# A relational graph layer: the first chunks in pieces, five halves by quarters, the bias spread by TensorE

## The reference

```python
masks = (relation[None] == rel_ids[:, None, None, None]).astype(x.dtype)
h = jnp.einsum('rbnm,bmd->rbnd', masks, x)
y = jnp.einsum('rbnd,rdo->bno', h, weight)
out = layernorm(x + y + bias)          # over the last axis
```

## Time and profile before

| what | value |
|---|---|
| three runs, median | 139.17 us (138.47 to 139.57) |
| profiled execution | 138.68 us |
| its span in the trace | 136.9 us |
| PE busy | 124.1 us, 91% |
| DVE busy | 85.8 us, 63% |
| ACT busy | 83.0 us, 61% |
| POOL busy | 69.2 us, 51% |
| DMA, mean over the span | 309 GB/s |

### The profile page before, as it was taken

How to read it: one execution, slowest core, us unless ns; L and a number is a source line. 1 busy time by engine, 2 the same in 40 slices (tenths; PEclk the granted TensorE clock), 3 DMA queues, 4 the chain that set the end, 5 groups by cost and what they waited for, 6 DMA issues and landing times.

```text
span 136.9 us, 2235 instructions
## 1 busy us (share of the span) xinstructions
PE 124.1 (91%) x727; PEld 77.2 (56%) x727; DVE 85.8 (63%) x270; ACT 83.0 (61%) x85; POOL 69.2 (51%) x79
## 2 busy tenths in 40 slices
PE   5986799489999999999999999999999999997920
PEld 2355688346564747465565656565656474666810
DVE  1185213765758494958677675757585939488851
ACT  3655753379785848484848586777758484513040
POOL 3000019975295709680786259553957195405440
PEclk9999999999999999999999999999999999999985
DMA  4999969999999999999999999999913000300422
GB/s 125 415 427 418 427 230 419 421 426 414 426 426 406 423 421 421 420 423 417 412 419 424 414 424 424 424 412 414 382 59 158 0 0 0 153 0 0 160 77 84
DMA packets 7789, 42.24 MB, mean 309 GB/s; under 512 B 864, under 2 KB 1376, under 8 KB 3936
## 3 DMA queue, kind: packets, MB, share of 16 engines
q1 hardware_dynamic: 7776, 42.08, 75.3%
HBM read 37.88 MB, written 4.19 MB: 307 GB/s over the span
## 4 chain that ended last, share of the span: by engine, by line
PE 73%; DMA 15%; SPq 4%; ACT 2%; DVE 1%; issue 1%; POOL 1%
PE h_ps L194 54%; DMA adj_sb<-in_adj_dram 15%; PE y_ps L201 10%; PE tp_ps L178 9%; ACT mask L171 1%; SPq L152 1%; SPq L258 1%; SPq L155 1%; POOL scale L219 1%; ACT h_sb L392 0%; DVE out_sb L223 0%; DVE stats L207 0%; ACT out_sb L398 0%; SPq L270 0%; SPq L269 0%
## 5 line engine op out<-in xcount | busy, mean ns | idle before, releaser
L171 ACT ACTIVATE mask<-adj_sb 128x2048 fp8e4<-128x2048 int32 x30 | 57.2, 1906 | 9.0 <-DMA adj_sb<-in_adj_dram 9.0
L194 PE MATMUL h_ps<-maskT,x_sb 128*128 128x512 fp8e4 (+1 forms) x152 | 32.0, 352 | 3.5 <-DVE maskT L182 2.5
L194 PE MATMUL h_ps<-maskT,x_fine 128*128 128x512 fp8e4 (+1 forms) x152 | 32.0, 352 | 0.4 <-DVE x_fine L164 0.4
L194 PE MATMUL h_ps<-maskT,x_rest 128*128 128x512 fp8e4 (+1 forms) x152 | 32.0, 352 | 0.1
L182 DVE COPY maskT<-tp_ps 128x512 uint32<-128x512 uint32 x30 | 20.6, 686 | 17.2 <-PE tp_ps L178 17.2
L167 POOL TENSOR_TENSOR x_bias<-x_sb,bias_sb 128x1024 f32<-128x1024 f32 x8 | 19.0, 2380 | 18.2 <-DMA bias_sb<-in_L_gnn_bias_dram 18.2
L194 PEld LDWEIGHTS h_ps<-maskT,x_sb 128*128 128x128 bf16 x152 | 14.3, 96 | 18.7 <-DVE maskT L182 2.9
L335 POOL TENSOR_SCALAR minus_mean<-mean_var 128x4 f32<-128x4 f32 (+1 forms) x16 | 3.1, 193 | 41.7 <-issue 22.9
L477 DVE TENSOR_TENSOR total<-y_ps,x_bias 128x512 f32<-128x512 f32 (+1 forms) x17 | 11.2, 660 | 20.2 <-issue 19.2
L386 ACT COPY h_sb<-h_ps 128x512 f32<-128x512 f32 x13 | 7.6, 585 | 23.4 <-issue 23.4
L178 PE MATMUL tp_ps<-identity,mask 128*128 128x128 f32 x128 | 21.1, 286 | 0.7 <-ACT mask L171 0.4
(11 more groups left out here) (28 smaller groups left out, 46.4 us busy)
## 6 DMA issues: line engine op xcount, KB each, us to landing
adj_sb<-in_adj_dram SPq DMA_DIRECT2D x30, 1024.0 KB, 17.6
x_sb<-in_x_dram SPq DMA_DIRECT2D x8, 512.0 KB, 17.9
out_dram<-out_sb SPq DMA_DIRECT2D x7, 512.0 KB, 7.7
adj_sb<-in_adj_dram SPq DMA_DIRECT2D x4, 512.0 KB, 5.2
out_dram<-out_sb SPq DMA_DIRECT2D x1, 256.0 KB, 2.0
out_dram<-out_sb SPq DMA_DIRECT2D x2, 128.0 KB, 1.8
bias_sb<-in_L_gnn_bias_dram SPq DMA_DIRECT2D x1, 64.0 KB, 14.8
w_sb<-in_L_gnn_weight_dram SPq DMA_DIRECT2D x1, 64.0 KB, 14.6
```

The lines of the kernel that those rows point to most:

```text
L171: nc.scalar.activation(mask[:, slot % NMASK], adj_sb[:, slot % NADJ], ACT.Copy, saturate=False).then_inc(done, 1)
L194: last = nc.tensor.matmul(h_ps[:, bank, 0:n], x_t, m_t, start=(part == 0 and t == 0), stop=(part == PARTS - 1 and t == TILES - 1))
```

## The change

It does seven things, all in the first third of the program:

1. The first 4 chunks, not 2, go in two pieces each (PIECED = 4).
2. The bias is loaded as one row, first thing after the first piece; PE multiplies it with a column of ones into `y_ps`, and ACT copies the result into `bias_sb`.
3. The x of batch 0 is split in halves of 4 tiles, and PE waits for each half.
4. The loads stand in another order: x of batch 1 and the weight follow chunk 3, x of batch 2 follows chunk 7.
5. Halves 0 to 4 (EARLY = 5), not 0 and 1, are multiplied by quarters. The turn of the next chunk stands between part 1 and part 2 of each chunk's products.
6. ACT, in these halves, copies quarter by quarter, with one convert between two copies.
7. Banks, evacuations and waits are renumbered to fit.

```diff
-    PIECED = 2
+    PIECED = 4
+    EARLY = 5
...
-        def take_rest(eng, x_slot, slot, done):
-            eng.tensor_tensor(x_rest[:, slot], x_sb[:, x_slot], upper(x_sb[:, x_slot]), ALU.subtract).then_inc(done, 1)
-
-        def take_fine(eng, slot, done):
-            eng.tensor_tensor(x_fine[:, slot], x_rest[:, slot], upper(x_rest[:, slot]), ALU.subtract).then_inc(done, 1)
+        def take_rest(eng, x_slot, slot, done, tiles=ALL):
+            eng.tensor_tensor(x_rest[:, slot, tiles], x_sb[:, x_slot, tiles], upper(x_sb[:, x_slot])[:, tiles],
+                              ALU.subtract).then_inc(done, 1)
+
+        def take_fine(eng, slot, done, tiles=ALL):
+            eng.tensor_tensor(x_fine[:, slot, tiles], x_rest[:, slot, tiles], upper(x_rest[:, slot])[:, tiles],
+                              ALU.subtract).then_inc(done, 1)
...
+        def part_products(part, x_slot, slot, places, bank, tiles=ALL):
             n = (places.stop - places.start) * O * P
-            for t in range(TILES):
+            for t in range(tiles.start, tiles.stop):
...
-            return (hf + 2 if hf > 1 else 2 * hf) % NBANK if c == 0 else (bank_of(hf) + c) % NBANK
+            return (CH * EARLY // 2 + hf - EARLY if hf >= EARLY else 2 * hf) % NBANK if c == 0 else (bank_of(hf) + c) % NBANK
...
             load_piece(0, 0)
+            sp.dma_start(bias_row[:, :], bias.unsqueeze(0)).then_inc(bias_loaded, 16)
             load_piece(0, 1)
             load_batch(0)
-            load_piece(1, 0)
-            load_piece(1, 1)
+            for u in range(1, PIECED):
+                for o in range(O):
+                    load_piece(u, o)
+            load_batch(1)
+            sp.dma_start(w_sb[:, 0, :], weight[0]).then_inc(weights_loaded, 16)
             for u in range(PIECED, UNITS):
                 load_unit(u)
-                if u == CH:
-                    sp.dma_start(bias_sb[:, :], bias.unsqueeze(0).to_broadcast([P, D])).then_inc(bias_loaded, 16)
-                    sp.dma_start(w_sb[:, 0, :], weight[0]).then_inc(weights_loaded, 16)
-                if u == 3:
-                    load_batch(1)
-                if u > 1 and u % CH == 1 and u // CH + 1 < B:
+                if u == 2 * CH - 1:
+                    load_batch(2)
+                if u > 2 * CH and u % CH == 1 and u // CH + 1 < B:
...
-            pool.wait_ge(bias_loaded, 16)
+            pool.wait_ge(bias_set, 1)
...
+            convert_piece(0, 0)
+            convert_piece(0, 1)
+            act.wait_ge(bias_spread, 1)
+            nc.scalar.copy(bias_sb[:, :], y_ps[:, 1, 0, :]).then_inc(bias_set, 1)
+            convert_piece(1, 0)
+            convert_piece(1, 1)
+            convert_piece(2, 0)
+            convert_piece(2, 1)
             copy_quarter(0, 0)
-            convert(3)
+            convert_piece(3, 0)
+            convert_piece(3, 1)
             copy_quarter(0, 1)
-            convert(4)
-            convert(5)
             copy_quarter(1, 0)
-            copy_quarter(1, 1)
-            convert(6)
-            convert(7)
-            finish_half(0)
-            convert(8)
-            for hf in range(2, HALVES - 1):
+            for u in range(CH, 2 * EARLY):
+                convert(u)
+                copy_quarter((u - 1) // 2, (u - 1) % 2)
+                if u > CH and u % 2 == 0:
+                    finish_half((u - 6) // 2)
+            convert(2 * EARLY)
+            convert(2 * EARLY + 1)
+            copy_quarter(EARLY - 1, 1)
+            convert(2 * EARLY + 2)
+            finish_half(EARLY - 3)
+            convert(2 * EARLY + 3)
+            finish_half(EARLY - 2)
+            convert(2 * EARLY + 4)
+            for hf in range(EARLY, HALVES - 1):
...
             empty_piece(0, 0)
+            dve.wait_ge(x_loaded[0], 16)
+            take_rest(nc.vector, 0, 0, rest_begun, HALF[0])
             empty_piece(0, 1)
-            dve.wait_ge(x_loaded[0], 16)
-            take_rest(nc.vector, 0, 0, rest_made)
+            take_rest(nc.vector, 0, 0, rest_made, HALF[1])
             collect_piece(0, 0)
+            dve.wait_ge(rest_begun, 1)
+            take_fine(nc.vector, 0, fine_begun, HALF[0])
             dve.wait_ge(rest_made, 1)
-            take_fine(nc.vector, 0, x_split)
+            take_fine(nc.vector, 0, x_split, HALF[1])
             empty_piece(1, 0)
             collect_piece(0, 1)
             empty_piece(1, 1)
             collect_piece(1, 0)
+            empty_piece(2, 0)
             collect_piece(1, 1)
-            for hf in range(HALVES - 1):
+            empty_piece(2, 1)
+            collect_piece(2, 0)
+            empty_piece(3, 0)
+            collect_piece(2, 1)
+            empty_piece(3, 1)
+            collect_piece(3, 0)
+            collect_piece(3, 1)
+            for hf in range(1, HALVES - 1):
...
+            def quarter_part(hf, c, part):
+                u, b = 2 * hf + c, hf // 2
+                if part == 0:
+                    wait_chunk(pe, piece_evacuated, evacuated, u)
+                    if NBANK <= u < 2 * EARLY:
+                        pe.wait_ge(h_copied, u - NBANK + 1)
+                if hf % 2 == 0 and c == 0:
+                    x_ready(part, b)
+                last = part_products(part, b % NX, b % 2, slice(u % NMT, u % NMT + 1), bank_of(hf, c))
+                if part == PARTS - 1:
+                    last.then_inc(multiplied, 1)
...
+            pe.wait_ge(bias_loaded, 16)
+            nc.tensor.matmul(y_ps[:, 1, 0, :], ones[0:1, :], bias_row[:, :], start=True, stop=True).then_inc(bias_spread, 1)
             keep_warm(2)
             turn_piece(0, 1)
             keep_warm(2)
-            products_quarter(0, 0)
+            quarter_part(0, 0, 0)
+            pe.wait_ge(rest_begun, 1)
+            part_products(1, 0, 0, slice(0, 1), bank_of(0), HALF[0])
+            pe.wait_ge(rest_made, 1)
+            part_products(1, 0, 0, slice(0, 1), bank_of(0), HALF[1])
             turn_piece(1, 0)
+            pe.wait_ge(fine_begun, 1)
+            part_products(2, 0, 0, slice(0, 1), bank_of(0), HALF[0])
+            pe.wait_ge(x_split, 1)
+            part_products(2, 0, 0, slice(0, 1), bank_of(0), HALF[1]).then_inc(multiplied, 1)
             turn_piece(1, 1)
-            products_quarter(0, 1)
-            turn(2)
-            products_quarter(1, 0)
-            turn(3)
+            for u in range(1, PIECED - 1):
+                quarter_part(u // 2, u % 2, 0)
+                turn_piece(u + 1, 0)
+                quarter_part(u // 2, u % 2, 1)
+                turn_piece(u + 1, 1)
+                quarter_part(u // 2, u % 2, 2)
             pe.wait_ge(weights_loaded, 16)
             project_half(0)
             products_quarter(1, 1)
-            turn(4)
-            turn(5)
-            for hf in range(2, HALVES - 1):
+            turn(CH)
+            for u in range(CH, 2 * EARLY - 1):
+                quarter_part(u // 2, u % 2, 0)
+                quarter_part(u // 2, u % 2, 1)
+                if u % 2 == 1:
+                    project_half((u - 3) // 2)
+                turn(u + 1)
+                quarter_part(u // 2, u % 2, 2)
+            quarter_part(EARLY - 1, 1, 0)
+            turn(2 * EARLY)
+            quarter_part(EARLY - 1, 1, 1)
+            project_half(EARLY - 2)
+            turn(2 * EARLY + 1)
+            quarter_part(EARLY - 1, 1, 2)
+            for hf in range(EARLY, HALVES - 1):
```

More of the change, by code:

```diff
@@ L102, in relational_layer @@
         collected = sem("collected")
+        rest_begun = sem("rest_begun")
+        fine_begun = sem("fine_begun")
         rest_made = sem("rest_made")
@@ L227, in bank_of, with last_in_bank @@
         def bank_of(hf, c=0):
-            return (hf + 2 if hf > 1 else 2 * hf) % NBANK if c == 0 else (bank_of(hf) + c) % NBANK
+            return (CH * EARLY // 2 + hf - EARLY if hf >= EARLY else 2 * hf) % NBANK if c == 0 else (bank_of(hf) + c) % NBANK
         def tp_bank(u, o=0):
             return (PIECED * O + u - PIECED if u >= PIECED else O * u + o) % NTP
+        def last_in_bank(u):
+            turned_before = PIECED * O + u - PIECED - NTP
+            return turned_before // O if turned_before < PIECED * O else u - NTP
         def gathered(u):
@@ L603, in turn @@
             def turn(u):
-                before = u - NTP if u >= PIECED + NTP else (u + 1 - PIECED) // O
                 pe.wait_ge(masked, u - PIECED + 1)
-                wait_chunk(pe, piece_evacuated, evacuated, before)
-                pe.wait_ge(collected, gathered(before + 1))
+                wait_chunk(pe, piece_evacuated, evacuated, last_in_bank(u))
+                pe.wait_ge(collected, gathered(last_in_bank(u) + 1))
                 turn_words(u % NMASK, tp_bank(u), range(O), turned)
@@ L613, in project_half @@
                     pe.wait_ge(added, 2 * (hf - 1))
+                else:
+                    pe.wait_ge(bias_set, 1)
                 project(lambda r: h_sb[:, hf % 2], y_ps[:, hf % 2], 1, HALF[0], projected, 2)
@@ L634, in products_half @@
```

(10 more changed lines are left out.)

20 lines of the change are left out of this document (9 added, 11 removed).

## The result

| | before | changed |
|---|---|---|
| median of 4 runs each | 139.37 us (138.47 to 140.01) | 142.76 us (142.42 to 142.99) |
| ratio, 95% interval | | 1.0246 (1.0184 to 1.0309) |
| profiled execution | 138.68 us, span 136.9 | 142.81 us, span 141.1 |

The changed kernel is 3.4 us slower by the medians and 4.1 by the two profiled executions. The prediction had the sign and the main mechanism, but 141.0 us, and its range ended at 142.0.

The account below looks back on a forecast made before the run. It took PE's progress when its gap-free stretch begins, after late loads, as the bound. Load gains go, ACT's waits come: turn of chunk 12 1.8+0.1 = 1.9 us later, 139.17+1.9, given as 141.0 us; range 139.3 to 142.0.

Parts of the forecast that it names:

- ACT's order holds the turns: Turns of chunks 7, 9, 10, 12: PE waits 1.40, 1.40, 1.54, 0.65 us for converts standing behind ACT's copies.
- the trough: DMA at 162 and 43 GB/s from 17 to 19 us, where the bias is due; costs 1.5 us, removed by one row.
- The first rival: Slow rows stay with the weight, so the load slowdown at 17 to 19 us remains there: 141.4 us, chance 0.1.
- At nothing I cost: Items given no time: bias product and copy, the row's SP queue time, earlier `x_bias`, the pieces of chunks 2 and 3.
- its 0.4 us on SP's queue: Issue of the bias row ahead of chunk 0's second piece: free, or first product 0.4 us later without cover.
- the walk: PE followed step by step through the new order: first product 8.0, chunk 1 11.9, chunk 4 23.3, turn of chunk 12 53.02.
- Rival (4): PE waits for the bias row ahead of the second piece; up to 1 us, 142.0 us, chance 0.03.
- `x_bias` earlier than 20.06: POOL's bias addition, at 20.06 us before, moves earlier; nobody waits for it, so it costs nothing.
- the slip between the weight load and the matmul row: Turn of chunk 12: predicted 53.02 was set against 51.22, a weight load's start, giving 1.9 us later with the cold start.
- a first product at 8.7: Late end for PE's first product, if x came only at 7.65; the walk took 8.0, the early end was 7.8.
- what the loads are worth: Bias as one row saves 1.5 us, moving x of batch 2 1.25; chunk 6 there at about 24.9, not 27.64.
- the 1.73 ahead of chunk 4: PE's 1.73 us standstill ahead of chunk 4's products, among the old waits expected mostly to go.

Follow-up runs that it names:

- a2_act_ahead: The changed kernel with ACT one convert further ahead in chunks 5 to 11, before the copy of the chunk two earlier: 138.5 us, ratio 0.9964.
- a4_both: The changed kernel with POOL's bias addition waiting for the split of x and ACT one convert ahead: 136.87 us, ratio 0.9826.
- c4_spread_by_dma: The changed kernel with the bias again spread over 128 partitions by DMA, behind chunk 4, without row, product or copy: 140.94 us, ratio 1.0156.
- b2_row_act_queue: The changed kernel with POOL's addition waiting, ACT one convert ahead and the bias row issued on ACT's DMA queue: 135.68 us, ratio 0.9789.
- b3_extra_row: The kernel before plus an unread one-row bias load behind the first piece, old broadcast kept: 138.98 us, ratio 1.0007.
- a1_bias_waits: The changed kernel, but POOL begins x_bias of batch 0 only when the three summands of x are made: 141.68 us, ratio 1.0167.
- a3_row_late: The changed kernel with the bias row loaded behind chunk 1's pieces and spread later, so x_bias also runs later: 140.21 us, ratio 1.0076.
- b4_before_row: The kernel before with the broadcast replaced by one bias row, loaded behind the pieces and spread by PE and ACT: 138.06 us, ratio 0.994.
- c1: The kernel before with the late bias row, and DVE's first add moved behind the evacuation of chunk 5: 137.46 us, ratio 0.9904.

## Why the prediction failed

**Right: ACT's order holds the turns.** Four waits, at the turns named, 1.33, 1.33, 1.49 and 0.41 us for 1.40, 1.40, 1.54 and 0.65. a2_act_ahead and a4_both show that they are the price: 4.3 and 4.8 us. The last was over-sized because half 5's products came 0.2 later than the rest of the walk, which is shorter waiting, not more time.

**Right: the trough was the bias's.** The changed kernel has none, c4_spread_by_dma has it where the broadcast is. The first rival (it stays with the weight) is false. The rule weighed there, from the Trainium skill, "DMA: Bandwidth & Descriptors", Specifications, that transfers of 512 B and more run at line rate, agrees with the trace for the weight's 128 rows. It does not for one row of 512 B read 128 times, 55 GB/s in the worst window of c4_spread_by_dma.

**Failed: "At nothing I cost".** Two of the items under these words hold the whole miss.

- *"its 0.4 us on SP's queue, ahead of the second piece (the DMA engines are busy with the first; without that cover the first product is 0.4 later)"*. The price was taken from the issue, and the cover from traffic. What it cost was neither: the loads behind it lost rate and came 1.2 us late, x of batch 0 among them (8.19 for 6.95). The second piece itself was on time. Rival (4) had a late row too, but as a wait of PE for the row; PE's product on it stood at 6.25, right behind the turn. Taking the row out of that place brings x 1.0 us forward and the end 0.5 to 1.2 (a4_both to b2_row_act_queue), and b3_extra_row shows the same dip in the other kernel.
- *"`x_bias` earlier than 20.06, which nobody waits for"*. True, and beside the point: an instruction that nobody waits for can still slow one that somebody does. It took the place beside `x_rest` (2.53 us for 0.68) and cost 1.1 to 1.6 us (a1_bias_waits, a4_both).

Together: 2.7 us by chunk 1, less 0.43 of smaller waits, plus the 0.2 ahead of half 5's products, 2.5 by the turn of chunk 12. The sum missed only 142.81-138.68-1.9 = 2.2, since the slip between the weight load and the matmul row had put 0.23 too much into it; that was luck. a3_row_late, without the two, follows the walk to 0.2 us; its turn of chunk 12 is 52.85-51.45 = 1.4 us later than the old one, with the cold start 1.5, and its span 1.5 longer. The range failed for the same reason: its ends came from the runs and from a first product at 8.7, while the delay of the loads and the place beside `x_rest` had no upper end at all.

**Half right: what the loads are worth.** "Whether it reaches the end depends on who waits for them" held. But I counted the 1.73 ahead of chunk 4 as a wait for loads; b4_before_row shows DVE's chain. So the trough alone was worth 0.8 us, not 1.5 (b4, ratio 0.994, 0.9896 to 0.9984), and 1.3 with DVE's step moved (c1, 0.9904). In the changed kernel this gain is fully spent on ACT's waits. With ACT a convert ahead, POOL's addition held back and the row on ACT's queue it comes out: 135.68 us, 2.1% below the kernel before (1.2 to 3.0%); with the late row instead 135.81, 2.4% (1.8 to 3.1%).

**Open.** Why a load of one row between the first two pieces takes rate from SP's stream, and behind the pieces or on ACT's queue doesn't. What lets TensorE reach its full pace at 4 to 7 us in eleven profiles and only at about 10 in a1, a2 and a4, at a recorded clock of 1.00; the changed kernel and b2_row_act_queue have an early row too and not the delay.

## What to carry to other kernels

Of every instruction that a change moves, ask not only who waits for it but what it now runs beside: an addition without a reader in sight on POOL made its neighbour on DVE nearly four times as long, most of that by the look of the rows a wait for the addition's end. A small load put first in a queue is priced by the traffic behind it, not by its own bytes; give it another queue, or put it behind the loads that something waits for. And when loads come early, look at once at the strictly ordered engine in the middle (here ACT): a convert issued one step ahead of the copy was worth 4.3 to 4.8 us.
